# First step sizes of a selective scan spread into the banks of the decay factors, a later table load, and other units for GpSimd's C products

## The reference

```python
def _mamba(x, inproj, conv_w, conv_b, xproj, dt_w, dt_b, Alog, Dp, outproj):
    xz = x @ inproj
    u, z = jnp.split(xz, 2, axis=-1)
    up = jnp.pad(u, ((0, 0), (K - 1, 0), (0, 0)))
    uc = conv_b
    for k in range(K):
        uc = uc + up[:, k:k + L, :] * conv_w[:, k]
    uc = jax.nn.silu(uc)
    dbl = uc @ xproj
    dt, Bm, Cm = jnp.split(dbl, [DT_RANK, DT_RANK + N], axis=-1)
    delta = jax.nn.softplus(dt @ dt_w + dt_b)
    A = -jnp.exp(Alog)
    def step(h, inp):
        u_t, d_t, B_t, C_t = inp
        dA = jnp.exp(d_t[..., None] * A)
        h = dA * h + (d_t * u_t)[..., None] * B_t[:, None, :]
        y_t = jnp.einsum('bdn,bn->bd', h, C_t)
        return (h, y_t)
    ...
    y = ys.transpose(1, 0, 2) + uc * Dp
    y = y * jax.nn.silu(z)
    return y @ outproj
```

## Time and profile before

| | us |
|---|---|
| median of 3 runs (1508.3 to 1510.53) | 1508.34 |
| the profiled execution, its own time | 1510.97 |
| its span | 1509.2 |
| VectorE busy, of the span | 1144.5 (76%) |
| TensorE busy | 1202.4 (80%) |
| GpSimd busy | 888.9 (59%) |
| ScalarE busy | 776.6 (51%) |

### The profile page before, as it was taken

The page is one execution under the profiler, slowest core; times in us unless marked ns, Lnnn a source line. Parts: engine busy times, 40 slices in busy tenths (PEclk is TensorE's granted clock), DMA queues, the critical chain, the costliest instruction groups (busy, mean ns, idle before and its releaser), DMA issues. The chain is left out here.

```text
span 1509.2 us, 14727 instructions
## 1 busy us (share of the span) xinstructions
PE 1202.4 (80%) x4972; PEld 670.6 (44%) x4972; DVE 1144.5 (76%) x1020; ACT 776.6 (51%) x1038; POOL 888.9 (59%) x395
## 2 busy tenths in 40 slices
PE   5899987698748897649887475473687999999998
PEld 4688842233203232113322121131246788787887
DVE  4433355999999999999999999999876544554544
ACT  5343456567546676545775555465255534343430
POOL 4420024999999999999999999999811000000000
PEclk9999999798868898769889788696798999999999
DMA  5133017322363342354223427312105030302012
GB/s 197 43 126 112 28 37 254 154 83 112 129 235 125 128 167 96 131 223 181 81 87 143 154 110 286 140 68 100 49 9 195 0 140 1 140 0 118 7 39 73
DMA packets 42544, 169.82 MB, mean 113 GB/s; under 512 B 5601, under 2 KB 10209, under 8 KB 30066
## 3 DMA queue, kind: packets, MB, share of 16 engines
q1 hardware_dynamic: 42482, 169.05, 30.2%
HBM read 136.53 MB, written 32.51 MB: 112 GB/s over the span
## 5 line engine op out<-in xcount | busy, mean ns | idle before, releaser
L1205 POOL TENSOR_TENSOR scan_dbu<-scan_rep,scan_bc 128x1024 f32<-128x1024 f32 x254 | 592.3, 2358 | 38.7 <-ACT scan_rep L1102 32.5
L1286 DVE TENSOR_TENSOR_SCAN scan_hs<-scan_hs,scan_dbu 128x1024 f32<-128x1024 f32 x189 | 432.2, 2287 | 15.7 <-ACT scan_hs L1131 14.1
L1131 ACT ACTIVATE scan_hs<-scan_rep,scan_neg_a 128x1024 f32<-128x1024 f32 x252 | 280.8, 1118 | 303.2 <-DVE scan_hc L1298 276.4
L1019 PE MATMUL scan_ysum<-scan_hc,scan_sel 128*32 128x512 f32 x1008 | 169.6, 804 | 208.5 <-DVE scan_hc L1298 193.1
L1298 DVE TENSOR_TENSOR scan_hc<-scan_hs,scan_bc 128x1024 f32<-128x1024 f32 x189 | 231.1, 1223 | 6.0
L1019 PEld LDWEIGHTS scan_ysum<-scan_hc,scan_sel 128*32 128x32 f32 x1008 | 35.3, 130 | 323.2 <-issue 269.5
L1211 POOL TENSOR_TENSOR scan_hc<-scan_hc,scan_bc 128x1024 f32<-128x1024 f32 x67 | 157.7, 2353 | 10.2 <-DVE scan_hc L1286 9.8
L1286 DVE TENSOR_TENSOR_SCAN scan_hc<-scan_hs,scan_dbu 128x1024 f32<-128x1024 f32 x67 | 152.7, 2279 | 2.0 <-POOL scan_dbu L1205 1.0
L899 PE MATMUL late_banks<-late_xin,scan_inwf 128*128 128x512 f32 x256 | 114.5, 601 | 0.0
L32 PE MATMUL ffn_sl<-ffn_tanh_s,xm_s 128*128 128x512 f32 x384 | 106.0, 411 | 2.3 <-DVE ffn_tanh_s L2031 2.3
L32 PE MATMUL moe_first<-moe_x_s,moe_w_s 128*128 128x512 f32 x384 | 98.3, 399 | 8.2 <-DVE moe_w_s L412 8.2
(11 more groups left out here) (234 smaller groups left out, 1732.0 us busy)
## 6 DMA issues: line engine op xcount, KB each, us to landing
scan_rep<-dd_rows SPq DMA_DIRECT2D x60, 1024.0 KB, 5.8
scan_bc<-bc_rows SPq DMA_DIRECT2D x32, 512.0 KB, 6.1
ffn_wt<-in_ew SPq DMA_DIRECT2D x16, 1024.0 KB, 7.3
dd_rows<-scan_dd SPq DMA_DIRECT2D x15, 1024.0 KB, 3.8
scan_inwf<-fold SPq DMA_DIRECT2D x12, 512.0 KB, 3.9
cond<-scan_bc SPq DMA_DIRECT2D x16, 256.0 KB, 3.1
y_all<-scan_yo SPq DMA_DIRECT2D x6, 512.0 KB, 3.1
scan_bc<-in_xT SPq DMA_DIRECT2D x4, 512.0 KB, 7.7
```

The costliest lines, as they stand in the source:

```text
L1019: mm = nc.tensor.matmul(ysum[i * D32:(i + 1) * D32, h, :], sel[:], hc[:, (s0 + i) % HCR, h * CT:(h + 1) * CT], start=False, stop=last, til ...
L1131: nc.scalar.activation(hs[:, s % HSR, :], rep[:, e % REPS, 0, :], ACT.Exp, scale=scale).then_inc(da_done, 1)
L1205: nc.gpsimd.tensor_tensor(dbu[:, s % DBR, :], rep[:, e % REPS, 1, :], bc[:, j, 0, :], ALU.mult).then_inc(dbu_done, 1)
L1286: nc.vector.tensor_tensor_scan(states, hs[:, s % HSR, :], dbu[:, s % DBR, :], 0.0, ALU.mult, ALU.add).then_inc(scan_done, 1)
```

## The change

1. The step sizes of the first period: ScalarE makes only Abs, Exp and Ln; VectorE takes the max with zero and adds in one instruction per half, from the PSUM banks.
2. TensorE spreads these step sizes straight into the two slots of `hs` (`spread_step`), and ScalarE makes the decay there in place, in one instruction of full width. Only the products still go through `pb` (`spread_du`). The order of the eight is `FIRST_SPREADS`. VectorE's first input product reads unit 0's product from `pb`.
3. The skip product of the first block goes ahead of the spreads; ScalarE does all first decays and copies ahead of its loop.
4. `neg_a`'s exponential moves from the start of the phase to behind the first Ln, its negation to behind VectorE's first product; the clearing of `u0` goes to GpSimd. A half of "t" waits only for its own half of "x".
5. GpSimd's C products are units 0, 6 and 11 in the first two periods, instead of 0, 4, 8 and 12.

```diff
-POOL_UNITS, LATE_POOL_UNITS = (0, 3, 7, 10, 13), (0, 4, 8, 12)
+FIRST_POOL_UNITS, POOL_UNITS, LATE_POOL_UNITS = (0, 6, 11), (0, 3, 7, 10, 13), (0, 4, 8, 12)
...
-    return r in (LATE_POOL_UNITS if late_step(s // UPP) else POOL_UNITS)
+    w = s // UPP
+    return r in (FIRST_POOL_UNITS if w < len(FIRST_POOL_UNITS) - 1 else LATE_POOL_UNITS if late_step(w) else POOL_UNITS)
...
-    [("t", 0, 0, h) for h in range(HALVES)] + [("r", i, kind, h) for i in range(NI) for kind in (1, 0) for h in range(HALVES)]
+    [("t", 0, 0, h) for h in range(HALVES)] + [("r", i, h) for i in range(NI) for h in range(HALVES)]
...
+FIRST_SPREADS = ((0, 0), (1, 0), (0, 1), (1, 1), (1, 2), (0, 2), (1, 3), (0, 3))
...
-                freed(pe, *(("x", k, i) for i in range(HALVES)))
+                freed(pe, ("x", k, h))
...
-            def replicate(i, kind, h):
-                out, done = claim(("r", i, kind, h))
-                pe.wait_ge((delta_done, du_done)[kind], 1)
-                nc.tensor.matmul(out, spread[:, i * P:(i + 1) * P],
-                                 dd[:, kind, h * CT:(h + 1) * CT], start=True, stop=True).then_inc(done, 1)
+            def spread_step(i):
+
+                if i >= HSR:
+                    wait_states(pe, i - HSR)
+                wait_delta(pe, 0)
+                for h in range(HALVES):
+                    mm = nc.tensor.matmul(hs[:, i % HSR, h * CT:(h + 1) * CT], spread[:, i * P:(i + 1) * P],
+                                          dd[:, 0, h * CT:(h + 1) * CT], start=True, stop=True)
+                mm.then_inc(spread_done, 1)
+
+            def spread_du(i):
+
+                pe.wait_ge(du_done, 1)
+                for h in range(HALVES):
+                    out, done = claim(("r", i, h))
+                    nc.tensor.matmul(out, spread[:, i * P:(i + 1) * P], dd[:, 1, h * CT:(h + 1) * CT], start=True, stop=True
+                                     ).then_inc(done, 1)
...
+            pe.wait_ge(soft, HALVES + 1)
+            skip(0, 0)
+            for kind, i in FIRST_SPREADS:
+                (spread_step, spread_du)[kind](i)
...
             def replica(i):
                 for h in range(HALVES):
-                    x, free = ready(act, "r", i, 1, h)
+                    x, free = ready(act, "r", i, h)
+                    if i == 0:
+                        act.wait_ge(dbu_done, 1)
...
-                    for h in range(HALVES):
-                        x, free = ready(act, "r", i, 0, h)
-                        nc.scalar.activation(hs[:, s % HSR, h * CT:(h + 1) * CT], x, ACT.Exp, scale=scale).then_inc(free, 1)
+                    act.wait_ge(spread_done, s + 1)
+                    nc.scalar.activation(hs[:, s % HSR, :], hs[:, s % HSR, :], ACT.Exp, scale=scale).then_inc(da_done, 1)
+                    return
...
-            nc.scalar.activation(neg_a[:], neg_a[:], ACT.Exp).then_inc(neg_done, 1)
             nc.scalar.preload_act_table_set("silu_and_others")
...
             step_ln(0)
+            nc.scalar.activation(neg_a[:], neg_a[:], ACT.Exp).then_inc(neg_done, 1)
             act.wait_ge(neg_done, 2)
+            for kind, i in FIRST_SPREADS:
+                (decay, replica)[kind](i)
...
+                if s == 0:
+                    x = [ready(dve, "r", 0, h)[0] for h in range(HALVES)]
+                    product = pb[:].rearrange("p h t -> p (h t)")
+                else:
+                    wait_du(dve, s)
+                    product = rep[:, s, 1, :]
+                nc.vector.tensor_tensor(dbu[:, s % DBR, :], product, bc[:, 0, 0, :], ALU.mult).then_inc(dbu_done, 1)
...
-            step_add(nc.vector, dve, 0)
+            dve.wait_ge(soft, HALVES + 2)
+            for h in range(HALVES):
+                x, free = ready(dve, "t", 0, 0, h)
+                own = dd[:, 0, h * CT:(h + 1) * CT]
+                nc.vector.scalar_tensor_tensor(own, x, 0.0, own, ALU.max, ALU.add).then_inc(free, 1)
             step_du(nc.vector, dve, 0)
+            dve.wait_ge(neg_done, 1)
+            nc.vector.tensor_scalar(neg_a[:], neg_a[:], -1.0, None, ALU.mult).then_inc(neg_done, 1)
```

More of the change, by code:

```diff
@@ L505, in own_adds @@
 def own_adds(w):
-    return sum(v == 0 or late_step(v - 1) for v in range(w + 1))
+    return sum(late_step(v - 1) for v in range(1, w + 1))
 DVE_INPUTS = 2
@@ L729, in wait_delta @@
         def wait_delta(eng, w):
-            if w == 0 or late_step(w - 1):
+            if w == 0:
+                freed(eng, *(("t", 0, 0, h) for h in range(HALVES)))
+            elif late_step(w - 1):
                 eng.wait_ge(delta_done, own_adds(w))
@@ L744, in wait_du @@
             if e < NI:
-                freed(eng, *(("r", e, 1, h) for h in range(HALVES)))
+                freed(eng, *(("r", e, h) for h in range(HALVES)))
             else:
                 eng.wait_ge(rep_in[e % REPS], 16 * (e // REPS + 1))
-        def wait_decay(eng, s):
-            if s < NI:
-                freed(eng, *(("r", s, 0, h) for h in range(HALVES)))
-            else:
-                eng.wait_ge(da_done, s + 1 - NI)
         def wait_hc(eng, s):
@@ L796, in load_rep @@
                     last = UPP * old_w + NI * (NJ - 1) + old_i
-                    wait_decay(sp, last)
+                    sp.wait_ge(da_done, last + 1)
                     sp.wait_ge(dbu_done, last + 1)
@@ L1033, in _ @@
                     step_size(*args)
-                elif kind == "r":
-                    if args == [0, 1, 0]:
-                        pe.wait_ge(consts_in, 3 * 16)
-                    replicate(*args)
-                elif args[-1] == 0:
+                elif kind == "x" and args[-1] == 0:
                     first_x_proj()
@@ L1045, in _ @@
                         for kind, *args in pe_chores(k, p, r):
-                            does[kind](*args)
+                            if [kind, *args] != ["skip", 0, 0]:
+                                does[kind](*args)
                         add_states(UPP * (DC * k + p) + NI * r)
@@ L1083, in step_in @@
                 if w == 1:
-                    for key in ((i, kind, h) for i in range(NI) for kind in range(2) for h in range(HALVES)):
-                        ready(act, "r", *key)
+                    act.wait_ge(spread_done, NI)
+                    for h in range(HALVES):
+                        ready(act, "r", NI - 1, h)
                 for h in range(HALVES):
@@ L1115, in decay @@
                 i, e = r % NI, NI * w + r % NI
-                if NI <= s < 2 * NI or w > 0 and r < NI:
-                    act.wait_ge(rep_in[e % REPS], 16 * (e // REPS + 1))
-                old = s - HSR
-                if old >= 0:
-                    if pool_unit(old):
-                        act.wait_ge(scan_done, old + 1)
-                    else:
-                        act.wait_ge(hc_done, by_dve(old + 1))
                 k, dc = divmod(w, DC)
@@ L1162, in _ @@
                 for r in range(UPP):
-                    if w == 0 and r < NI:
-                        replica(r)
-                    decay(UPP * w + r)
+                    if UPP * w + r >= NI:
+                        decay(UPP * w + r)
                     if w + 1 < PERIODS and r == step_in_at:
@@ L1293, in weigh @@
                 if s == HCR - 1:
-                    freed(dve, *(("r", i, kind, h) for i in range(NI) for kind in range(2) for h in range(HALVES)))
+                    dve.wait_ge(spread_done, NI)
+                    for h in range(HALVES):
+                        ready(dve, "r", NI - 1, h)
                 if w % DC == 0:
@@ L1299, in weigh @@
                                         ).then_inc(hc_done, 1)
-            dve.wait_ge(neg_done, 1)
-            nc.vector.tensor_scalar(neg_a[:], neg_a[:], -1.0, None, ALU.mult).then_inc(neg_done, 1)
-            nc.vector.memset(u0[:, :, 0:TAPS - 1], 0.0).then_inc(u0_zeroed, 1)
-            dve.wait_ge(u0_zeroed, 1)
+            dve.wait_ge(zeroed, 2)
             for i, (dc, lo, hi) in enumerate(FIRST_TAPS):
```

25 lines of the change are left out of this document (19 added, 6 removed).

## The result

The changed kernel takes 1516.84 us, the median of 5 runs (1514.76 to 1518.59), against 1508.34; the ratio is 1.0047, interval 1.0035 to 1.0060. It is slower, by 8.5 us between the medians and by about 7 us by the ratio. In a later measurement (e5), with 12 runs of it and 34 of the kernel before, the ratio was 1.0031 (1.0016 to 1.0047). The profiled execution has a span of 1515.6 us, 6.4 more than that of the kernel before. The other 2.1 us between the medians are those of the two profiled executions within their own runs: the one before took 1510.97, 2.6 above its median, the one after 1517.34, 0.5 above.

A forecast was written before the change was run, and what follows sets the result against it. VectorE was taken to carry the selective scan, GpSimd just behind. Terms: -3.2 us in the front, +3.3 at unit 17, +0.1 behind, so +0.2 on 1508.34: 1508.5, range 1505.2 to 1511.6.

The forecast's parts named there:

- the lead given back at unit 17: Second period: the 3.2 us lead is lost in one 3.3 us wait on ScalarE's decay; unit 17 at 299.9 against 299.79.
- After that nothing is changed: Everything behind scan 32, which was put at +0.2: no further gain or loss.
- The front: Serial work before the first recurrence: -3.2 us in the sum; first recurrence at about 237.2 instead of 240.69.
- (a): Start of ScalarE: neg_a's exponential and its table load leave, moving VectorE's chain 0.7 us earlier, bounds 0 and 0.9.
- (b): Step sizes on ScalarE: two Relus go, saving 0.8 us, bounds 0.5 and 0.96; logarithm ends at 230.45.
- (c): Sum and max on VectorE become two half-width operations from PSUM: 1.50 us against 1.22, counted as +0.3.
- (d): TensorE spreads step sizes first, into the decay banks: unit 0's step 232.05 to 234.0, its product to 235.9.
- (e): VectorE reads unit 0's product from PSUM in 1.22 us; first recurrence at about 237.2 instead of 240.69.
- GpSimd's list: Unit 11's product is the 17th instruction from unit 3's input, 2.313 us each: 246.7 to 286.05.
- Sums and projection: TensorE, units 8 to 11: start at 286.05, take 10.64 us, 1.7 more as bound; projection ends at 296.7.
- the rival of the low clock: TensorE at low clock: first spreads 1.6 us more, sums of units 8 to 11 1.7 more; both 1511.8; chance 0.21.
- Unit 21: Second period: VectorE's 1.34 us wait before it is filled by unit 20's product (1.17); stays at about +0.1.

The follow-up runs named there:

- e5: The changed kernel once more, unaltered, with a profile of its own: median 1516.91 us against 1511.43 for the kernel before, ratio 1.0031.
- e4: The kernel before plus 0.91 us of clearing on VectorE ahead of the first step sizes, nothing else: ratio 1.0016.
- e6: The changed kernel, with TensorE filling its waits in the last group with products by a zero matrix: ratio 1.0026.
- e2: The kernel before with only GpSimd's C products of the first two periods changed to units 0, 6 and 11: ratio 1.0019.
- e3: The changed kernel with unit 9 in the place of unit 11 among GpSimd's C products of the first two periods: ratio 0.9994.
- e10: The kernel before plus 3.6 us of clearing on VectorE ahead of the first step sizes: ratio 1.0017.
- e12: The changed kernel with ScalarE making unit 17's decay ahead of the convolution eviction instead of behind it: ratio 0.9969.
- e11: The changed kernel with GpSimd's C products of the first two periods at units 0, 5, 9 and 12: 1506.65 us against 1512.76, ratio 0.9958.
- e7: The changed kernel with GpSimd's C products as before and TensorE's zero-matrix filling in every scan quarter without a projection: ratio 1.0026.
- e1: The changed kernel with GpSimd's C products of all periods at units 0, 4, 8 and 12, as before; the rest kept: ratio 0.9967.

## Why the prediction was wrong

It said 1508.5 and 1505.2 to 1511.6, no change; it was 1516.84. The mechanism that it put first, the lead given back at unit 17, is the one that the trace shows. The step that failed is the sentence "After that nothing is changed", with the term of zero that it gave to all that lies behind unit 32: measured, the lag grew there from 1.6 us at unit 33 to 5.9 at unit 255 and 6.5 at the end of the span. Up to unit 33 the forecast was off by 1.4 us (+1.6 for +0.2), within its range. The last 2.1 us of the 8.5 lie in the base: its median over these few runs, 1508.34, is lower than those on the chips of the experiments (1510.16 to 1512.76), while the changed kernel's came again (1516.91). The prediction took the base as it was; whether its low median is chance or the chip isn't shown.

**The front.** Forecast -3.2 to -3.5, measured -2.1 at unit 0. (a) and (b) held: VectorE adds the first step sizes 1.6 us earlier by the block's clock (230.26, against 231.98), forecast 1.5. (c) held: the two halves and the hand-over take 1.38 us, 0.13 more than before, where 0.3 was forecast. (d) was too good: from the step sizes to unit 0's product in the banks it gave 3.9 us, and it took 5.6. TensorE's skip product, put ahead of the spreads, ran at the low clock and kept them waiting; the stretches of the skip and of the spreads in the changed kernel, by engine and granted clock:

```profile
229.28:232.83 3.55, 3.55 (x5) 1.48 (x5) 2.48 (x4) 1.15 (x2) 0.00 (x0) 0.50 0.93 343
232.83:235.14 2.31, 2.31 (x6) 1.06 (x5) 0.17 (x2) 0.00 (x0) 0.00 (x0) 0.74 0.94 300
```

The step sizes were there at 231.6 instead of 232.0, the spreads began at 232.83, and unit 0's product was in the banks at 237.15 instead of 235.9. By unit 3's input on GpSimd the lead was 2.5 us (247.36, against 249.94), where 3.2 was forecast. (e), the product read from PSUM, took 1.23 us, as forecast. The Trainium skill (VectorE: DVE Perf Modes, the section on the TRN2 errata) would have it 0.065 us longer than one from SBUF; the 1.23 here beside the 1.22 of the earlier trace rows do not show that.

**GpSimd's list.** Forecast 17 instructions and 39.35 us from unit 3's input to the end of unit 11's product; 247.36 to 286.72 is 39.36.

**Sums and projection.** Forecast 10.64 us, with up to 1.7 more. Measured 286.87 to 298.35, 11.48, of which the sums ran at 0.50; their stretch in the changed kernel:

```profile
286.87:290.44 3.57, 3.57 (x17) 0.66 (x17) 3.27 (x2) 1.12 (x1) 3.57 (x2) 0.50 0.74 264
```

The Trainium skill (TensorE: Matmul & The Clock Gate, the section on HAM oscillation) says that a burst behind a wait starts at half rate. Here it does, behind 5.09 us of idle; the sums at 993.30 in the kernel before, behind 2.28 us of idle, ran at 1.00.

**Unit 17.** From the eviction to the recurrence 3.15 us were forecast and 3.15 measured. The lag of 1.8 in the place of 0.1 is the front's missing 0.7 (a lead of 2.5 at unit 3's input, not 3.2), 0.15 between the end of GpSimd's product and the sums, and the 0.84 of sums and projection. The first and the last are the two prices of the rival of the low clock, each about half of what it allowed. With the lag of unit 17 alone the kernel would have been at about 1510.2. Unit 21 went as forecast, its wait of 1.34 us filled.

**Behind unit 17.** I took a delayed scan for a shifted scan. The lag went from +1.8 to +0.5 at unit 193 and to +5.9 at unit 255, and e4 shows the same course from a delay alone. The two largest pieces, 1.65 and 2.75 us, are TensorE's sums and totals at the lower clock, measured in the profile. That the clock is their cause is read from the granted clock, from the equal sums, and from the eleven profiles that fall into two kinds by it between units 225 and 233. It wasn't isolated by an experiment, since keeping TensorE busy (e6) delayed the same work by as much. Between units 33 and 193 lies a gain, of about 1 us here and of 5 to 7 in e2, e3, e10 and e12. Its largest common piece, 1.8 us in each of them and here, is a place where the profile of the kernel before meets the low clock: from unit 113 to unit 117 it takes 15.81 us, the other ten profiles without filling 13.99 to 14.05. TensorE's gate projection there, before and after:

```profile
622.26 5.94 PE L956 MATMUL late_banks<-late_xin,scan_inwz 128*128 128x512 f32 x8 [0.56 <-ACT scan_dd L1089]
```

```profile
625.04 3.70 PE L972 MATMUL late_banks<-late_xin,scan_inwz 128*128 128x512 f32 x8 [1.36 <-ACT scan_dd L1109]
```

ScalarE makes unit 117's decay behind the gates, and VectorE waits for it 2.18 us before and 0.35 after. The rest of the gain, and the 0.6 us behind the scan, I haven't taken apart.

The chances were wrong accordingly. The profile before had waits of VectorE on ScalarE's decays all through the scan (19 of them from 240.69 to 1100, 14.1 us in all), and the granted clock of that stretch was 0.82; from these a range behind unit 32 should have been drawn. Of a lag of 2.0 us at unit 17 the scan made 5.7 in e4, and e3 lost 0.6 of a lead of 2.0: a range of 4 us to either side is what these runs would give.

## What to carry to other kernels

When a product changes engines, look at where it stands in the new engine's list and at who waits for the whole group that it belongs to, not at the two engines' loads: unit 11's place in GpSimd's list cost 4 us at unit 17 (e3). The load counts as well, but less: with the same front, three products on GpSimd (e3) were 1.1 us behind four (e11) at unit 17, and 3.3 at unit 33. In a pipeline that several engines set in turns, a lead or a lag isn't carried to the end as it is; measure it at landmarks along the trace, in more than one execution, and compare against the same kernel with a plain delay (e4) before blaming an instruction. And a queue that has 0.03 us of slack in the profile is the first place to look, even if no row names a wait there.

## What the runs showed of the hardware that had not been expected

The time of this kernel depends on when its work comes, by 4 us and more: a delay of 0.91 us on VectorE moved the last recurrence of the profiled execution by 5.7 us (e4). The same sums of 16 records took 1.92 us where the granted clock was 1.00 and 3.64 where it was 0.50. A faster piece went with a slower one behind it: the gate projection at full clock (3.60 us) left TensorE idle for 3.98 us, and the sums behind it ran at 0.50; at a mixed clock (4.79 us) it left 2.28 us of idle, and the sums ran at 1.00. Raising the mean clock from 0.889 to 0.957 with idle products made the kernel slower (e7, 1.0026, where the same kernel without them, e1, had 0.9967), though the Trainium skill (TensorE: Matmul & The Clock Gate, the section on HAM oscillation) advises arranging the work so that the array stays warm. Here the filling stood ahead of sums that another engine waited for. And a second profile of the same kernel repeated the course of the first to 0.3 us from unit 17 on (e5), while its runs spread over 11 us; a single median of a few runs shows neither.
